# One PSUM bank for turned probabilities, and a second one for out-projection products, in a fused cross-attention and spline-layer kernel

## The reference, cut to what matters

```python
x = x + xattn(layernorm(x), ctx, seg)     # 16 heads of 128, plus a rotary part of 64
x = x + spline_layer(layernorm(x))        # routing to 64 tiles, piecewise linear per tile
# xattn:
kv_c, q_c = kv @ W_kvc, q @ W_dq          # 256 and 384 wide
scores = (q_nope @ k_nope.T + q_rope @ k_rope.T) * scale   # masked to 9 keys by seg
out = softmax(scores) @ (kv_c @ W_uv)     # per head
return out @ W_o
```

## Time and profile before

| | us |
|---|---|
| median of 3 runs | 3238.69 (3235.26 to 3240.01) |
| profiled execution | 3238.15 |
| its span, first to last instruction | 3236.4 |
| TensorE busy | 3069.6 (95% of the span) |
| weight loads of TensorE | 2386.5 (74%) |
| VectorE busy | 2083.3 (64%) |
| ScalarE busy | 1490.6 (46%) |
| DMA, mean over 16 engines | 44% |

### The profile page before, as it was taken

The page is one execution under the profiler, slowest core; times in us unless marked ns, Lnnn a source line. Parts: engine busy times, 40 slices in busy tenths (PEclk is TensorE's granted clock), DMA queues, the critical chain, the costliest instruction groups (busy, mean ns, idle before and its releaser), DMA issues.

```text
span 3236.4 us, 39942 instructions
## 1 busy us (share of the span) xinstructions
PE 3069.6 (95%) x13890; PEld 2386.5 (74%) x13890; DVE 2083.3 (64%) x4440; ACT 1490.6 (46%) x2907; POOL 714.7 (22%) x516
## 2 busy tenths in 40 slices
PE   7999999999999999999999999999999999999924
PEld 4788768887788867888678876888678876888722
DVE  2555537775577746777377764777467763777687
ACT  2655525553445435445264543555345452555411
POOL 5222241112211131110411113111311113111046
PEclk9999999999999999999999999999999999999955
DMA  6554444444534445433454444444454444544301
GB/s 205 195 172 160 173 163 164 136 140 148 192 121 140 140 156 189 134 128 130 156 193 140 140 146 172 141 140 140 141 181 140 140 131 150 186 140 137 118 27 4
DMA packets 170054, 473.34 MB, mean 146 GB/s; under 512 B 33136, under 2 KB 61424, under 8 KB 149248
## 3 DMA queue, kind: packets, MB, share of 16 engines
q1 hardware_dynamic: 164784, 469.91, 43.7%
q0 software_dynamic: 5072, 0.88, 0.6%
HBM read 369.84 MB, written 67.31 MB: 135 GB/s over the span
## 4 chain that ended last, share of the span: by engine, by line
PE 83%; DVE 7%; issue 4%; ACT 3%; POOL 2%; DMA 1%; SPq 0%; DVEq 0%; ACTq 0%; POOLq 0%
PE psC L1934 18%; PE psD L1927 10%; PE psA L1864 8%; PE psT L1916 6%; PE psA L1833 5%; PE psB L1873 5%; PE psD L1884 4%; PE psS L1901 3%; PE psB L1833 3%; PE psS L1907 3%; PE psS L1903 3%; PE psS L1902 3%; PE psS L1904 3%; PE psA L1855 2%; PE psB L1855 2%
## 5 line engine op out<-in xcount | busy, mean ns | idle before, releaser
L1934 PE MATMUL psC<-w_o_pair,attn_hi 128*128 128x512 f32 x1920 | 638.4, 413 | 18.7 <-DVE acc L1342 10.8
L1033 ACT ACTIVATE exps_ring<-exps_ring,neg_max 128x512 f32<-128x512 f32 x512 | 370.8, 724 | 424.9 <-DVE neg_max L1314 424.9
L1314 DVE CUSTOM_DVE_ANT_0 exps_ring<-psS,mask 128x512 f32<-128x512 f32 x512 | 353.2, 690 | 294.4 <-PE psS L1907 289.1
L1044 ACT ACTIVATE probsT_hi<-psT 128x512 fp32r<-128x512 f32 x512 | 305.8, 599 | 364.9 <-PE psT L1916 363.3
L1934 PEld LDWEIGHTS psC<-w_o_pair,attn_hi 128*128 128x128 f32 x1920 | 332.2, 189 | 89.5 <-DVE acc L1342 24.9
L1039 ACT ACTIVATE exps_ring<-exps_ring,row_sum_inverse 128x512 f32<-128x512 f32 x512 | 369.6, 722 | 61.0 <-DVE row_sum_inverse L1320 61.0
L1326 DVE TENSOR_TENSOR probsT_lo<-psT,probsT_hi 128x512 fp32r<-128x512 f32 x512 | 350.6, 686 | 58.3 <-ACT probsT_hi L1044 56.6
L1934 PE MATMUL psC<-w_o_pair,attn_lo 128*128 128x512 f32 x960 | 379.4, 395 | 0.0
L1342 DVE TENSOR_TENSOR acc<-acc,psC 128x512 f32<-128x512 f32 x448 | 303.2, 677 | 17.3 <-PE psC L1934 11.4
L1916 PE MATMUL psT<-ident,exps_ring 128*128 128x128 f32 x2048 | 305.0, 272 | 0.0
L1916 PEld LDWEIGHTS psT<-ident,exps_ring 128*128 128x128 f32 x2048 | 252.8, 139 | 66.4 <-issue 2.1
(11 more groups left out here) (301 smaller groups left out, 5497.8 us busy)
## 6 DMA issues: line engine op xcount, KB each, us to landing
w_o_pair<-w_o_split SPq DMA_DIRECT2D x112, 1024.0 KB, 5.4
w_uq_ring<-w_uq_split SPq DMA_DIRECT2D x114, 384.0 KB, 3.5
w_uv_quad<-w_uv_split SPq DMA_DIRECT2D x29, 1024.0 KB, 5.0
w_uk_ring<-w_uk_split SPq DMA_DIRECT2D x114, 256.0 KB, 2.8
w_qr_sorted<-w_qr_split SPq DMA_DIRECT2D x29, 768.0 KB, 4.3
x_stage<-in_x_dram SPq DMA_DIRECT2D x32, 512.0 KB, 5.9
x_stage<-in_ctx_dram SPq DMA_DIRECT2D x32, 512.0 KB, 4.1
acc<-in_x_dram SPq DMA_DIRECT2D x32, 512.0 KB, 5.3
```

Source lines behind the costliest of these rows:

```text
L1033: act.activation(E[:, qt, :], E[:, qt, :], ACT.Exp, scale=-1.0, bias=mx[:, i % 2, qt:qt + 1], accum_out=rs[:, i % 2, qt:qt + 1]).then_inc( ...
L1044: act.activation(PT[0][:, :, qt * P:(qt + 1) * P], psT[qt % 2][:, :].rearrange("p (c n) -> p c n", c=TT), ACT.Copy)\
L1314: dve.tensor_tensor_reduce(E[:, qt, :], psS[qt % 2][:, :], mask[:, qt, :], -SCALE, BIG, ALU.add, ALU.min, mx[:, i % 2, qt:qt + 1]).then_in ...
L1934: mm_ = pe.matmul(ps[:, :], attn[a][:, 2 * pair + i, t * P:(t + 1) * P], WO[:, half, o, i, :], start=i + a + o == 0, stop=i + a == 2)
```

## The change

The two banks of turned tiles become psT and psE. Turned tiles go to psT; in the first quad, the odd tiles of heads 0 and 1 and the second tile of head 2 go to psE. A turned tile waits for the remainder copy of the tile before it, or of the one before that if the tile before went to the other bank. Out-projection products with odd `w` go to psE, those with even `w` stay in psC. In quads 1 to 3 value tile 1 goes to psE, the others to psD. The waits of `load_o` and `wo_hi`, of the transposed input of the next batch and of the one-hot transposes at the end follow. At a batch's end product 7 is put ahead of the second transposed stage on TensorE, and its add ahead of `norm_stats` on VectorE.

```diff
@@ -44,9 +44,10 @@
 
     A0, AQ = 4, 1 + HQ
     B0, BQ = 3, 1 + HQ
-    DQ = TT + HQ
+    DQ = TT - 1 + HQ
     PAIRS = H // 2
-    AN, BN, CN, DN = A0 + NQ * AQ, B0 + NQ * BQ, 8 * PAIRS - TT + TT // 2, NQ * DQ + TT // 2
+    AN, BN, CN, DN = A0 + NQ * AQ, B0 + NQ * BQ, TT // 2 + 4 * PAIRS, NQ * DQ - 1 + TT
+    EN = 4 * (PAIRS - 1) + NQ - 1
     TN = 4 * TT
 
     def pos_a(b, q, k):
@@ -62,16 +63,19 @@
     def pos_v(b, q, kt):
         if q == 0:
             return b * (CN if kt % 2 else DN) + kt // 2
-        return b * DN + q * DQ + kt - TT // 2
+        if kt == 1:
+            return b * EN + (2 * q - 1) * 4 + q - 1
+        return b * DN + q * DQ - 1 + (0 if kt == 0 else kt - 1)
 
     def pos_av(b, q, i):
         return b * DN + q * DQ + TT // 2 + i
 
     def pos_o(b, q, pair, w):
-        return b * CN + TT // 2 + (2 * q + pair) * 8 + w
+        n = 2 * q + pair
+        return b * EN + n * 4 + q + pair + w // 2 if w % 2 else b * CN + TT // 2 + n * 4 + w // 2
 
     def pos_end(b, t):
-        return b * CN + TT // 2 + 8 * (PAIRS - 1) + t, b * DN + NQ * DQ - TT // 2 + t
+        return b * CN + TT // 2 + 4 * (PAIRS - 1) + t, b * DN + NQ * DQ - 1 + t
 
     def rope_no(b, q):
         return b * (NQ + 1) + (0 if q == 0 else 1 + q)
@@ -97,8 +101,8 @@
 
 
         psS = [bank("psS0"), bank("psS1")]
-        psT = [bank("psT0"), bank("psT1")]
-        stages = [psS[0], psS[1], psT[0], psT[1]]
+        psT, psE = bank("psT"), bank("psE")
+        stages = [psS[0], psS[1], psT, psE]
         psA, psB, psC, psD = bank("psA"), bank("psB"), bank("psC"), bank("psD")
 
 
@@ -248,6 +252,7 @@
         s_acc = sem("acc_in")
         fullA, fullB, fullC, fullD = sem("fullA"), sem("fullB"), sem("fullC"), sem("fullD")
         freeA, freeB, freeC, freeD = sem("freeA"), sem("freeB"), sem("freeC"), sem("freeD")
+        fullE, freeE = sem("fullE"), sem("freeE")
         fullT, freeT = sem("stage_turned"), sem("stage_copied")
         s_turn, s_pthi, s_ptlo = sem("probs_turned"), sem("probsT_hi_done"), sem("probsT_lo_done")
         s_S, s_sm, s_exp, s_prob = sem("scores"), sem("scores_masked"), sem("exps"), sem("probs_done")
@@ -322,9 +327,20 @@
         rampi = E[:, 3, 320:384].bitcast(I32)
 
         def values_bank(q, kt):
-            return (psC, fullC, freeC) if q == 0 and kt % 2 else (psD, fullD, freeD)
-
-        psTb = [p[:, :].bitcast(BF16) for p in psT]
+            if q == 0:
+                return (psC, fullC, freeC) if kt % 2 else (psD, fullD, freeD)
+            return (psE, fullE, freeE) if kt == 1 else (psD, fullD, freeD)
+
+        def turn_in_e(q, i, qt):
+            return q == 0 and qt % 2 == 1 and (i < 2 or (i == 2 and qt == 1))
+
+        def turn_bank(q, i, qt):
+            return psE if turn_in_e(q, i, qt) else psT
+
+        def out_bank(w):
+            return (psE, fullE, freeE) if w % 2 else (psC, fullC, freeC)
+
+        psTb = [p[:, :].bitcast(BF16) for p in (psT, psE)]
 
         def onehot_wide():
             return oh[:, :].rearrange("p (t a) -> p t a", a=1).broadcast_to([P, NT, SLICE])
@@ -462,7 +478,7 @@
                     sp.wait_ge(fullC, b * CN)
                     sp.wait_ge(fullD, b * DN)
                 else:
-                    sp.wait_ge(fullC, pos_o(b, q, pair, 0) - 4 + 4 * half)
+                    sp.wait_ge(fullE, pos_o(b, (n - 1) // 2, (n - 1) % 2, 3 + 4 * half) + 1)
                 sp.dma_start(WO[:, half].rearrange("p s i n -> p (s i n)").bitcast(F32),
                              flat(wo_dram[bass.ds(n, 1), half])).then_inc(s_wo[half], 16)
 
@@ -1042,7 +1058,7 @@
             def turned(b, q, i, qt):
                 act.wait_ge(s_turn, tile_no(b, q, i, qt) + 1)
                 act.activation(PT[0][:, :, qt * P:(qt + 1) * P],
-                               psT[qt % 2][:, :].rearrange("p (c n) -> p c n", c=TT), ACT.Copy)\
+                               turn_bank(q, i, qt)[:, :].rearrange("p (c n) -> p c n", c=TT), ACT.Copy)\
                    .then_inc(s_pthi, 1)
 
             def attended(b, q, i):
@@ -1054,7 +1070,7 @@
                 n = q * 2 + pair
                 act.wait_ge(s_wor[half], 16 * (n + 1))
                 if not (q == 0 and pair == 0):
-                    act.wait_ge(fullC, pos_o(0, q, pair, 0) - 4 + 4 * half)
+                    act.wait_ge(fullE, pos_o(0, (n - 1) // 2, (n - 1) % 2, 3 + 4 * half) + 1)
                     act.wait_ge(s_wos[half], 16 * n)
                 act.activation(WO[:, half, 0], wo_raw(q, pair, half), ACT.Copy)\
                    .then_inc(s_woh, 1)
@@ -1324,7 +1340,7 @@
                 dve.wait_ge(s_pthi, tile_no(b, q, i, qt) + 1)
                 hi = PT[0][:, :, qt * P:(qt + 1) * P]
                 dve.tensor_tensor(PT[1][:, :, qt * P:(qt + 1) * P],
-                                  psT[qt % 2][:, :].rearrange("p (c n) -> p c n", c=TT),
+                                  turn_bank(q, i, qt)[:, :].rearrange("p (c n) -> p c n", c=TT),
                                   hi.bitcast(F32), ALU.subtract).then_inc(s_ptlo, 1)
 
             def attended_lo(b, q, i):
@@ -1337,9 +1353,10 @@
                 half, t = w // TT, w % TT
                 if first_add:
                     dve.wait_ge(s_acc, 16 * TT * (b + 1))
-                dve.wait_ge(fullC, pos_o(b, q, pair, w) + 1)
+                ps, full, free = out_bank(w)
+                dve.wait_ge(full, pos_o(b, q, pair, w) + 1)
                 a = acc[:, t, half * HALF:(half + 1) * HALF]
-                dve.tensor_tensor(a, a, psC[:, :], ALU.add).then_inc(freeC, 1)
+                dve.tensor_tensor(a, a, ps[:, :], ALU.add).then_inc(free, 1)
 
             def add_end(b, t, half):
 
@@ -1598,10 +1615,9 @@
                 add_out(b, NQ - 1, 0, 5)
                 turned_lo(b, NQ - 1, HQ - 1, 3)
                 add_out(b, NQ - 1, 0, 6)
+                add_out(b, NQ - 1, 0, 7)
                 if not last:
                     norm_stats(b + 1, 2)
-                add_out(b, NQ - 1, 0, 7)
-                if not last:
                     norm_x(b + 1, 2)
                 attended_lo(b, NQ - 1, HQ - 1)
                 for t in range(TT):
@@ -1815,8 +1831,10 @@
                         pe.wait_ge(freeT, b * TN + k - 3)
                     elif k < 2 and not (b == 0):
                         pe.wait_ge(s_sm, b * H * TT - 1 + k)
+                    elif k == 2 and not (b == 0):
+                        pe.wait_ge(s_ptlo, b * H * TT)
                     elif not (b == 0):
-                        pe.wait_ge(s_ptlo, b * H * TT - 3 + k)
+                        pe.wait_ge(freeE, b * EN)
                     for c in range(4):
                         blk = 4 * half + c
                         mm_ = pe.transpose(stages[k % 4][:, c * P:(c + 1) * P],
@@ -1910,10 +1928,14 @@
 
                 n = tile_no(b, q, i, qt)
                 pe.wait_ge(s_prob, n + 1)
-                if not (n < 2):
-                    pe.wait_ge(s_ptlo, n - 1)
+                ps = turn_bank(q, i, qt)
+                last = (q, i, qt - 1) if qt > 0 else (q, i - 1, TT - 1)
+                beside = (i > 0 or qt > 0) and turn_in_e(q, i, qt) != turn_in_e(*last)
+                done = n - 1 if beside else n
+                if done > 0:
+                    pe.wait_ge(s_ptlo, done)
                 for c in range(TT):
-                    mm_ = pe.transpose(psT[qt % 2][:, c * P:(c + 1) * P], E[:, qt, c * P:(c + 1) * P], ident)
+                    mm_ = pe.transpose(ps[:, c * P:(c + 1) * P], E[:, qt, c * P:(c + 1) * P], ident)
                 mm_.then_inc(s_turn, 1)
 
             def attend(b, q, i):
@@ -1922,6 +1944,8 @@
                 pe.wait_ge(freeD, pos_av(b, q, i))
                 if q == 0 and i == 0:
                     pe.wait_ge(freeC, pos_v(b, 0, TT - 1) + 1)
+                elif i == 0:
+                    pe.wait_ge(freeE, pos_v(b, q, 1) + 1)
                 for kt in range(TT):
                     for v, p in ((0, 0), (0, 1), (1, 0)):
                         mm_ = pe.matmul(psD[:, :], V[v][:, kt, i * P:(i + 1) * P], PT[p][:, kt, :],
@@ -1941,8 +1965,11 @@
                     pe.wait_ge(s_wo[half], 16 * ((b * NQ + q) * 2 + pair + 1))
                 if w == 0:
                     pe.wait_ge(freeD, pos_av(b, q, 2 * pair + 1) + 1)
-                wait_free(freeC, pos_o(b, q, pair, w))
-                project(psC, pair, half, t).then_inc(fullC, 1)
+                ps, full, free = out_bank(w)
+                wait_free(free, pos_o(b, q, pair, w))
+                if q == 0 and pair == 0 and w == 1:
+                    pe.wait_ge(s_ptlo, tile_no(b, 0, 2, 1) + 1)
+                project(ps, pair, half, t).then_inc(full, 1)
 
             def out_end(b, t, half):
                 if t == 0:
@@ -2057,9 +2084,9 @@
                 out_proj(b, NQ - 1, 0, 5)
                 turn_probs(b, NQ - 1, HQ - 1, 3)
                 out_proj(b, NQ - 1, 0, 6)
+                out_proj(b, NQ - 1, 0, 7)
                 if not last:
```

(5 more changed lines are left out.)

## The result

The changed kernel takes 3197.16 us (median of 4 runs, 3196.37 to 3198.95) against 3237.57 for the kernel before (4 runs, 3235.26 to 3240.01): ratio 0.9876, 95% interval 0.9859 to 0.9893. The forecast was 3207 with the range 3200 to 3219, so the sign and the order of size were right, and the gain was 40.4 us where 31.4 were forecast, outside the range. The profiled execution took 3196.37 us.

What follows compares the result with a forecast made beforehand. TensorE was busy 95% of the span, so only its standstills could be won. Terms 21.8 + 5.9 + 3.5 - 1.4 + 1.6 = 31.4 us off the profiled 3238.15, adjusted to the median, gave 3207, range 3200 to 3219.

Steps and rivals of the forecast that it cites:

- value tile, 24 quads: Value tiles 1 and 2 of a quad stop waiting for VectorE's remainder copies: 24 x (0.76 + 0.15) = 21.8 us gained.
- pairs, 49 places: At third turned tiles the product's 0.18 us wait goes, 0.06 appears at the turned tile: 49 x 0.12 = 5.9 us gained.
- long reduction, 7 places: Where VectorE's long reduction delays copies, the product's 1.23 us wait goes, the fourth tile waits 0.7 to 0.77: 3.5 us gained.
- ends 2 to 7, third tile included: Between batches, the next batch's stage waits for product 7's add: 0.2 us lost per end, -1.4 us over seven ends.
- last batch's end: No next stage follows, so more product waits go, less 0.35 us each at third and fourth tiles: 1.6 us gained.
- first batch's end: End of the first batch, priced like the other six: 0.2 us lost to the stage's wait for product 7's add.
- The failed term: At third turned tiles, a weight load about 0.15 us late has some 0.09 hidden, leaving 0.06 us on the path.
- The wait for the add at the stage: At each batch end, the next batch's stage transposes in psE wait 0.6 to 0.8 us for product 7's add.
- The wait only changes place: Rival: turned tiles wait as long as the products did, so the gain is 22.3 us, giving 3216; chance 16%.
- The value gain: Rival: VectorE or ScalarE becomes the next limit in the same head, only the other 9.6 us remain: 3229; chance 7%.
- The slower rival: First tile's copies come later, so second tiles wait in 104 heads: 18 us lost, 3225, or 88 us, 3295; chance 4%.
- The clock: Rival: new waits at the other six batch ends bring half clock there, 10 us back, 3217; chance 5%.

Runs made afterwards that it cites:

- experiment 2: Changed kernel with all out-projection products back in psC, keeping the single bank for turned tiles and value tile 1 in psE: 3215.28 us, ratio 0.9932.
- experiment 9: Changed kernel with the remainder copy of a head's second turned tile made twice in 104 heads: 3244.32 us, ratio 1.0021 against the kernel before.
- experiment 8: Changed kernel with the remainder copy of a head's first turned tile made twice in 104 heads: 3202.16 us, ratio 0.9893 against the kernel before.
- experiment 3: Changed kernel with value tile 1 back in psD, keeping odd products in psE and the new batch-end order: 3222.04 us, ratio 0.9952.
- experiment 6: Changed kernel with the second half of the second transposed stage in psC and norm_stats ahead of product 7's add: 3195.83 us, ratio 0.9874.

## Why the prediction was right or wrong

The terms of the sum against the rows of the profiled executions, in us (the start's -0.4 and a few single places of up to 0.4 are left out):

| step | forecast | measured |
|---|---|---|
| value tile, 24 quads | 21.8 | 23.0 |
| pairs, 49 places | 5.9 | 49 x 0.20 = 9.8 |
| long reduction, 7 places | 3.5 | 7 x 0.59 = 4.1 |
| ends 2 to 7, third tile included | -1.2 | 1.3 - 6 x 0.27 = -0.3 |
| last batch's end | 1.6 | 0.3 - 0.27 + 1.45 = 1.5 |
| first batch's end | -0.2 | 4.0 - 0.27 = 3.7 |
| sum | 31.4 | 41.8 |

- **Value tile: right**, place, mechanism and size; experiment 2 gives 22.3 (with the single bank, which alone is worth nothing).
- **The failed term: "The load runs one matmul (0.23) ahead of its own and needs 0.58 / 4 = 0.15, which hides some 0.09: 0.06 on the path."** The lateness of the load was right (0.17, forecast 0.11 to 0.18). What it costs was not. 0.15 is not the time that a load needs: the loads of a late group follow each other faster (0.42 us for the four), and a late one is used as little as 0.03 us after its start. So 0.22 or 0.23 less 0.03 is hidden, the third tiles, 0.17 late, cost nothing, and each pair gives the whole of its wait. The same 0.2 at every kind of place: 1.02 late costs 0.83 (long reduction), 0.47 (0.51 less 0.04) costs 0.27 (last head's third tile; forecast 0.42 and 0.35), 0.90 costs 0.70 (experiment 9), 0.20 costs 0 to 0.02 and 0.27 costs 0.07 (experiment 8). It makes 3.9 us on the pairs. The high bound, +0.18 each, took the bracket of the product's wait for the whole of it and was too low as well: 0.20 was measured.
- **The missed step: the first batch's end**, put down as one of seven like ends. It is not like the others: an input tile's transfer sets it, and the kernel before lost half-clock time there, in both its profiles. The prediction had read that stretch only as a threat for the other ends and not as a loss that could go. 1.1 of the 4.0 us is the shorter idle time of the loader, about 1.6 the half clock (3.2 to 3.4 us at half pace), and 1.1 the wait for a context tile (1.27 against 0.15). None of the three is shown to come from the change: profiles with the changed banks have first ends from 80.9 to 83.7 us, and three of them have half clock and waits of 0.9 to 1.4 there (experiments 3, 6 and 8). So this part may be luck of the executions that were profiled. It matters for the range: without the 4.0 us the time would have been some 3201, just inside it.
- **Ends and tail:** right within 1 us. The wait for the add at the stage is there (0.58 against a forecast of 0.6 to 0.8).
- **The rivals.** "The wait only changes place" was right of the loader (73 waits, 23.9 us against 24.5) and wrong of the time: the new place has a cover that the old one lacked. The value gain was not overtaken: 2.60 us of VectorE's idle time are still there. The slower rival's copies were not late by themselves, and its price was set too high by the same wrong term, 0.09 hidden in place of 0.2 (5 to 8 us, not 18). The clock did not fall at more ends.
- **What the profile after would show:** the rows came as named, with the loader's 0.1 us being 0.17 (0.21 in the bracket) and its 0.7 to 0.8 being 1.02 (TensorE now comes to that place 0.2 earlier, and VectorE does not), but for one. TensorE's busy time was to stay nearly the same and fell by 24.

**Open.** Why the input tile's transfer takes 6.6 us in both profiles of the kernel before and 5.7 in the changed one. All other variants show 5.7 as well, the single bank alone among them (its first end: 82.11), so it is not the products or the value tile that do it. Half clock at the first end appears in 7 of the 14 profiles. In those with it the loader had been idle for 2.75 to 3.85 us, in those without for 2.00 to 2.80, so idle time of 2.75 to 2.80 is seen with either. Why a context tile's transfer, issued at the same place of its end, lands after 4.2 us in one and after 6.3 in another is not known either. Profiles with half clock have first ends of 82.3 to 86.0 us, those without 80.9 to 82.9. Whether unprofiled runs share it was not measured.

## What to carry to other kernels

A wait in a list is not yet a price: look at what stands between the late weight load and its matmul, and at which place a wait can be taken free. When a resource is scarce, take it from the user whose next fill finds it free, or late by less than that cover, and give it to the one whose wait stands bare; and price each user from its own margin (0.57 us here) and not by a rule about rotation. Stages that repeat are priced once, but the first and the last of them are looked at by themselves. And before two profiles' sums are compared, the waits for transfers that differ from one execution to the next are taken off.

## What the runs showed of the hardware

- A weight load of a group of four transposes (128x128, fp32) may be some 0.2 us late without moving a matmul: it starts 0.22 or 0.23 us ahead of its matmul when nothing holds it, 0.05 to 0.08 ahead when it is 0.17 late and 0.03 ahead when it is later than 0.2, and the group's loads take 0.42 to 0.44 us in place of 0.59.
- From the end of VectorE's remainder copy to the start of the load that it releases: 0.11 to 0.12 us (1480.31 to 1480.43, 1502.16 to 1502.27); from the end of an add: 0.05 (388.95 to 389.00).
- Of 41.8 us less span, 24.0 came out of TensorE's busy time at the same number of matmuls, at most 1.7 of it by half clock: busy time holds part of the stalls.
- The last context tile of a batch (512 KB) lands 4.2 to 6.3 us after its issue, in ends 2 to 7 of the 14 profiles; the weight loader waits up to 1.6 us for it, or not at all.
- The Trainium skill (Perfetto Trace Analysis, "Matmuls") asks for rotation of banks between independent groups; here giving up the rotation of the turned tiles made a ratio of 1.0003 [0.9994, 1.0013], and giving one to the value tile won 22 us.
